# Offsets and masks spread over the partitions: by DMA from DRAM in fp32, or by matmuls on three bf16 parts

## Chip, cores and metric

One core of one Trainium2 chip runs the kernel. The metric is device time in microseconds, the median over several executions. All tensors are fp32 except where another type is named.

## What is computed

The input x is (8, 64, 16, 16). Two stages follow each other, each with a group normalisation of 32 groups and a residual.

```python
x = x + local_attention(_gn(x))        # 3x3 windows, 8 heads, a gate
x = x + relu(_mdcn(_gn(x)))            # modulated deformable 3x3 convolution
# _mdcn: om = conv3x3(x, w_om) + b_om  -> 108 rows: dy, dx, mask for 4 groups x 9 taps
py = h - 1 + ki + dy ; px = w - 1 + kj + dx
v  = bilinear(x[group], py, px) * sigmoid(mask)
out = einsum('ogck,bgckhw->bohw', w_dcn, v)
```

The change is in the second stage.

## The kernel before

Each engine has its own program; they meet at semaphores. The first stage ends at about 50 us, and the second normalisation and the offset convolutions follow.

**Offsets.** The convolution that gives offsets and masks runs in five pieces (`PIECES`: one image, one image, then two images each), six tap steps each (`convolve`, L1167), and leaves 108 rows in PSUM: 36 mask rows, 36 y rows and 36 x rows. ACT takes a piece out with its bias and puts tanh of half the mask rows in place (`offsets`, L592 and L594). DVE cuts the piece into three bf16 parts whose sum is the fp32 value, and takes the largest magnitude (`offset_part`, L876 to L886). SP stacks the three parts of a kind under one another in `stack_x`, `stack_y`, `stack_m` (L384 to L391).

**Sampling without a gather.** A sample is a product of hat functions: haty(row distance) times hatx(column distance). For every image i of 8 and every tap m of 9 (step t = 9 i + m, 72 steps) there are
- `select_x` (PE, L1232): for two taps at once, the x offset of each deformable group on its partitions, by a 0/1 matrix `selx` against the stacked parts, which also adds the column's own position. It goes to PSUM bank 5. ACT makes the hat from it, Abs (L628) and then Relu of 1 minus it (L630), into one of `HX` = 6 buffers.
- `select_y` (PE, L1218): the same for y, three slices an image (one, two and two pairs of taps), into PSUM bank 7; then Abs (L615) and Relu (L620) on ACT, and on 64 partitions the low half of an fp16 split on POOL (`low_y`, L478, L481, L485; the very first slice on DVE).
- `spread_mask` (PE, L1201 and L1207): the masks, six slices for each two images, into bank 7, and a copy out of it by ACT (L606).
- `spread_y` (PE, L1247): the y hats of the step, spread over the 128 partitions as three quarters of 256 columns, in two column halves, into banks 0 and 1 or 2 and 3 by turns.
- `multiply` (DVE, L915): the spread rows times the column weights, 768 columns, into one of 12 places of `smp`.

**Products.** Products of `smp` with the transposed image windows (PE, `block_of_products`, L1273, banks 4 and 6) sum up the samples; DVE multiplies them with the mask (`values`, L929, three parts an image), the weights are applied by `final` (PE, L1316), and DVE finishes an image (L942, L936). SP sends it out.

**Order.** The order on each engine is written out by hand in `sampling`. On PE, step t first does the spread of step t + 1, then select_x on even t, then blocks of products at m = 6, 7, 8 of the image and m = 0, 2, 3 of the next, the convolution of piece 3 within image 0 and of piece 4 within image 3 (`LAST_CONV`), window transposes, select_y for the next image at m = 2, 6, 8, mask slices where `MASKS` says so, and `final` at m = 5. Bank 7 is shared by select_y and the mask slices, and `bank7_free` waits for ACT to have taken the last one out. ACT follows the same order.

**If offsets are large**, further passes follow with other rows; in the run shown `choice` gives one pass.

Of the kernel before, what the change touches and what calls it, by code (L numbers as in the profile page):

```python
# [12 lines left out]
TAPS = 9  # L13
# [8 lines left out]
OM = 3 * DG * TAPS  # L22
ND = DG * TAPS
STACK = 3 * ND
# [25 lines left out]
UNITS = T // 2  # L50
HX = 6
LEAD = 2
SIDE = STRIPS // 2
# [13 lines left out]
MSLOT = 3 * BANK + 3 * HW  # L67

MASKS = [{4: (0, 0), 5: (0, 1), 7: (0, 2)}, {0: (0, 3), 1: (0, 4), 3: (0, 5), 5: (1, 0), 7: (1, 1)},
         {0: (1, 2), 3: (1, 3), 5: (1, 4), 7: (1, 5)}, {0: (2, 0), 3: (2, 1), 5: (2, 2), 7: (2, 3)},  # L70
         {0: (2, 4), 3: (2, 5)}, {0: (3, 0), 3: (3, 1), 5: (3, 2), 7: (3, 3)}, {0: (3, 4), 3: (3, 5)}, {}]


PIECES = [(0, 0, HW), (0, HW, BANK), (1, 0, BANK), (2, 0, BANK), (3, 0, BANK)]
PIECE_OF = {0: 0, 1: 1, 2: 2, 4: 3, 6: 4}
CONV_BANK = [4, 0, 6, 6, 4]
PAIRS_AT = {(0, m): (2 + m, 4) for m in range(6)} | {(1, 2): (8, 6)}
PARTS_AT = {(0, m + 1): (2, m) for m in range(5)} | {(1, m + 2): (3, m) for m in range(5)} | {(4, m): (4, m) for m in range(5)}
# [3 lines left out]
CHUNK, VALS, SLICES = 3, 3, 6  # L82
# [9 lines left out]


def seventh(i, m):

    at = i * STEPS + m - 1
    while at >= 0:
        i, m = divmod(at, STEPS)
        if m in SEL_Y and i + 1 < B:
            return "y", 3 * (i + 1) + SEL_Y[m] + 1  # L100
        if m in MASKS[i]:
            c, part = MASKS[i][m]
            return "m", SLICES * c + part + 1
        at -= 1
    return "y", 3


def bass_local_attention_then_deformable_conv(nc, x, cf, wom, sel16, rows16, out):
# [8 lines left out]
    with ExitStack() as ctx:  # L117
# [19 lines left out]
        selx = sb("selx", [STACK + 2, TAPS * P], bf16)  # L137
        own = sb("own_group", [P, DG])
        shiftbias = sb("shiftbias", [P, SHIFTS])
        sely = sb("s_sely", [STACK + 2, PAIRS * P], bf16)  # L140
        selm = sb("s_selm", [STACK + 2, 3 * P + 3 * C], bf16)
# [20 lines left out]

        conv_words = sb("conv_staged", [P, TAPSTEPS * OM + 2 * PAD])
        v = views(conv_words, ("womt", TAPSTEPS * OM), ("dup0", PAD), ("dup1", PAD))
        womt, dup = v["womt"], [v["dup0"], v["dup1"]]

        x_words = sb("x_parts", [P, 2 * N + P + 3 * BANK + BANK])
        v = views(x_words, ("xin", N), ("x2", N), ("beyond", P), ("parts", 3 * BANK), ("rest", BANK))
# [56 lines left out]
        def group_mask(rows):  # L225

            return own[:, :].unsqueeze(1).unsqueeze(3).to_broadcast([P, rows, DG, W])
# [119 lines left out]
        def _(sp):  # L347
# [33 lines left out]
            for p, piece in enumerate(PIECES):  # L381
# [10 lines left out]
                if p == 1:  # L392
                    odd_pairs(0)
# [1152 lines left out]
```

## Time and profile before

| | |
|---|---|
| median of 3 runs | 194.14 us (194.06 to 194.34) |
| the profiled execution's own time | 194.37 us |
| its span, first to last instruction | 192.4 us |
| PE busy | 171.5 us, 89% |
| DVE busy | 152.3 us, 79% |
| ACT busy | 103.8 us, 54% |
| POOL busy | 86.6 us, 45% |
| moved by DMA | 7.66 MB |
| granted TensorE clock, mean | 0.999 |

The span leaves out about 2 us around the instructions. PE is TensorE, DVE VectorE, ACT ScalarE, POOL GpSimd, SP the engine that issues most DMAs. A share of busy time is an average over stages with different limits, so the stretches of the sampling are read one by one. PE's busy time counts overlapping matmuls from first to last; the chain of waits tells what a group of them adds to the path.

### The profile page before, as it was taken

What the parts mean: (1) busy time and instruction counts of PE and PEld (TensorE: products, weight loads), DVE (VectorE), ACT (ScalarE), POOL (GpSimd) and SP (SyncE); (2) the same over time, 40 slices, a digit from 0 to 9 for tenths busy, and PEclk for the clock granted to TensorE, in tenths of its full rate; (3) what the DMA queues carried; (4) which work ended last, traced back from release to release, by engine and by line L of the source; (5) the groups of instructions that cost most, each with busy time, mean ns of one, the idle gap of its engine ahead of it and who ended that gap; (6) DMA issues with size and microseconds to landing.
All of it is one profiled execution on the core that took longest, in us unless ns stands there. A gap on an engine that the chain in (4) does not pass through costs nothing.

```text
span 192.4 us, 4617 instructions
## 1 busy us (share of the span) xinstructions
PE 171.5 (89%) x1818; PEld 119.0 (62%) x1818; DVE 152.3 (79%) x258; ACT 103.8 (54%) x195; POOL 86.6 (45%) x103
## 2 busy tenths in 40 slices
PE   0598888979799989999989999999889999999990
PEld 0234434634257535557777999467668888998870
DVE  3999889993869789966889988428998897979920
ACT  1165086400007795559848878367848868686000
POOL 8608971974023076505806627304624617545000
PEclk9999999999999999999999999999999999999999
DMA  5951000000030114018141000000011100000001
GB/s 171 313 90 14 3 0 0 3 0 0 18 91 12 30 32 117 13 46 217 27 118 49 0 3 3 0 0 0 13 38 49 33 19 3 0 17 2 20 0 24
DMA packets 10325, 7.66 MB, mean 40 GB/s; under 512 B 5175, under 2 KB 8773, under 8 KB 10297
## 3 DMA queue, kind: packets, MB, share of 16 engines
q1 hardware_dynamic: 10201, 7.24, 14.7%
q8 instruction: 16, 0.26, 0.6%
q14 instruction: 12, 0.10, 0.2%
q0 software_dynamic: 96, 0.06, 0.1%
HBM read 2.82 MB, written 0.52 MB: 17 GB/s over the span
## 4 chain that ended last, share of the span: by engine, by line
PE 62%; DVE 17%; ACT 9%; issue 4%; DMA 3%; POOL 2%; SPq 0%; DVEq 0%; POOLq 0%
PE ps L1273 20%; PE ps L1247 11%; PE ps L1167 10%; PE ps L1316 6%; DVE smp_prod L778 4%; DVE smp_prod L804 3%; PE ps L1232 3%; PE ps L1099 3%; DMA kept<-in_cf 3%; PE ps L1218 2%; ACT disty L615 2%; PE ps L1184 2%; ACT haty L620 1%; PE ps L1027 1%; ACT hx_selx L628 1%
## 5 line engine op out<-in xcount | busy, mean ns | idle before, releaser
L915 DVE TENSOR_TENSOR smp_prod<-ps,hx_selx 128x768 f32<-128x768 f32 x72 | 67.4, 952 | 10.0 <-PE ps L1247 9.2
L1273 PE MATMUL ps<-smp_prod,windows_attention 128*64 128x192 f32 (+2 forms) x512 | 54.9, 337 | 0.1
L1273 PEld LDWEIGHTS ps<-smp_prod,windows_attention 128*64 128x64 f32 x512 | 38.3, 136 | 5.8 <-DVE windows_attention L900 0.4
L1247 PE MATMUL ps<-haty,by_rows 128*64 128x256 f16 x432 | 39.1, 274 | 1.3 <-DVE smp_prod L915 1.2
L478 POOL TENSOR_SCALAR disty<-disty 64x512 f32<-64x512 f32 (+1 forms) x23 | 14.0, 610 | 57.6 <-ACT haty L620 57.6
L1247 PEld LDWEIGHTS ps<-haty,by_rows 128*64 128x64 f16 x432 | 26.6, 109 | 6.4 <-issue 2.7
L628 ACT ACTIVATE hx_selx<-ps 128x512 f32<-128x512 f32 x36 | 21.3, 591 | 16.2 <-PE ps L1232 16.2
L485 POOL TENSOR_TENSOR haty<-disty,haty 64x512 f16<-64x512 f32 (+1 forms) x23 | 24.0, 1042 | 1.9
L1167 PE MATMUL ps<-conv_staged 128*108 128x512 f32 (+1 forms) x60 | 23.3, 521 | 0.8 <-ACT x_parts L592 0.6
L630 ACT ACTIVATE hx_selx<-hx_selx 128x512 f32<-128x512 f32 x36 | 22.7, 631 | 1.1
L929 DVE TENSOR_TENSOR vals_attw<-ps,windows_attention 128x384 f32<-128x384 f32 x24 | 13.3, 555 | 7.4 <-PE ps L1273 4.4
L615 ACT ACTIVATE disty<-ps 128x512 f32<-128x512 f32 (+1 forms) x24 | 12.5, 520 | 8.0 <-PE ps L1218 7.3
L1232 PE MATMUL ps<-stack_x,selx 110*64 110x256 bf16 x144 | 16.3, 272 | 0.0
L481 POOL TENSOR_SCALAR disty<-disty 64x512 f32<-64x512 f32 (+1 forms) x23 | 14.7, 638 | 1.9
L1167 PEld LDWEIGHTS ps<-conv_staged 128*108 128x108 f32 x60 | 9.5, 172 | 8.1 <-issue 5.9
L620 ACT ACTIVATE haty<-disty 128x512 f16<-128x512 f32 (+1 forms) x24 | 13.4, 559 | 0.8
L606 ACT COPY windows_attention<-ps 128x512 f32<-128x512 f32 (+1 forms) x24 | 11.2, 467 | 4.8 <-PE ps L1201 2.7
L592 ACT ACTIVATE x_parts<-ps,kept 108x256 f32<-108x256 f32 (+1 forms) x3 | 1.6, 538 | 21.9 <-PE ps L1167 21.9
L449 POOL TENSOR_TENSOR smp_prod<-smp_prod 128x1024 f32<-128x1024 f32 x4 | 9.3, 2357 | 6.0 <-DVE smp_prod L804 6.0
L1099 PE MATMUL ps<-smp_prod,kept 128*128 128x512 f32 x20 | 9.6, 611 | 1.6 <-POOL smp_prod L449 1.6
L804 DVE TENSOR_TENSOR smp_prod<-ps,windows_attention 128x1024 f32<-128x1024 f32 x9 | 10.5, 1213 | 0.1
L1232 PEld LDWEIGHTS ps<-stack_x,selx 110*64 110x64 bf16 x144 | 10.3, 110 | 0.0
(138 smaller groups left out, 244.5 us busy)
## 6 DMA issues: line engine op xcount, KB each, us to landing
windows_attention<-windows_attention SPq DMA_DIRECT2D x8, 256.0 KB, 3.8
x_parts<-in_x SPq DMA_DIRECT2D x2, 256.0 KB, 3.1
bcast<-in_bcast SPq DMA_DIRECT2D x2, 256.0 KB, 7.0
x2seq<-x_parts SPq DMA_DIRECT2D x4, 128.0 KB, 2.5
out<-x_parts SPq DMA_DIRECT2D x16, 32.0 KB, 2.0
vals_attw<-in_cf SPq DMA_DIRECT2D x1, 480.0 KB, 5.9
stack_m<-x_parts SPq DMA_DIRECT2D x12, 36.0 KB
kept<-in_cf SPq DMA_DIRECT2D x1, 390.5 KB, 5.2
```

What stands on the lines that cost most here:

```text
L485: nc.gpsimd.tensor_tensor(hi, d, hi, ALU.add).then_inc(s_loy, 1)
L615: nc.scalar.activation(d, bank(7)[:, 0:w], ACT.Abs).then_inc(s_absy, 1)
L620: nc.scalar.activation(haty[i % 2][:, YP[e] * HW:YP[e] * HW + w], d, ACT.Relu, bias=1.0, scale=-1.0).then_inc(s_hiy, 1)
L628: nc.scalar.activation(h, bank(5), ACT.Abs).then_inc(s_absx, 1)
L630: nc.scalar.activation(h, h, ACT.Relu, bias=1.0, scale=-1.0).then_inc(s_hatx, 1)
L804: nc.vector.tensor_tensor(grid(prod[:, t * N:(t + 1) * N]), grid(bank(PB[pos % 3], 2)), shifted(vpad, t), ALU.mult).then_inc(s_pv, 1)
L915: nc.vector.tensor_tensor(pairs, rows, cols.unsqueeze(1).to_broadcast([P, QUARTERS, HW]), ALU.mult).then_inc(s_mult, 1)
L1099: ins = nc.tensor.matmul(bank(2 + c), ident, prod[:, t * N + c * BANK:][:, 0:BANK], start=(t == 0), stop=(t == 6))
L1167: ins = nc.tensor.matmul(bank(CONV_BANK[p])[0:OM, lo:hi], womt[:, k * OM:(k + 1) * OM], shifted(dup[h], 3 * ky + 2 * single)[:, j:j + (hi ...
L1232: ins = nc.tensor.matmul(bank(5)[h * C:(h + 1) * C, k * HW:(k + 1) * HW], selx[:, tap * P + h * C:tap * P + (h + 1) * C], stack["x"][:, i ...
L1247: ins = nc.tensor.matmul(ps[h * C:(h + 1) * C, at:at + HW], by_matrix(a, QUARTERS - 1 - k)[:, h * C:(h + 1) * C], haty[i % 2][:, p * HW:(p ...
L1273: return nc.tensor.matmul(dst[:, at:at + strips * 3 * SP].rearrange("p (s k n) -> p s k n", k=3, n=SP), rows, sampled(i, ki, m, first, str ...
```

## The change

The three bf16 parts, the stacks, the select matmuls and the mask matmuls are taken out.
- The convolution's weights are put in another order on POOL (`womo`), so that its rows come out as 36 mask rows, 40 y rows (two parities of taps, four groups, five pairs) and 36 x rows, 112 in all (`PLACED`). DVE adds the position of the sample (`where`, `shiftcol`, the bias for the first two pieces, straight from PSUM) in fp32 (`place`).
- SP writes the rows to a DRAM tensor `placed_rows`, waits for that write, and reads them back with a source that repeats, so that each row lands on all the partitions that need it: `expand_x` (three taps, 128 x 768), `expand_y` (one image, 128 x 1280), `expand_masks` (one image, four transfers of 64 partitions). For the masks of the first two images there is an extra write after ACT.
- ACT's Abs reads these tiles, with a bias per partition for what depends on the partition; units of x have three taps, four buffers. Mask rows hold tanh + 1, and the final weights are halved.
- Banks 4, 5 and 7 come free of the selects: `spread_y` goes through three pairs of banks (`SPREADS`) and runs two steps ahead (`AHEAD`).
- The order on partitions in windows and by_rows changes from group by column to column by group.
- Piece 4 is convolved in bank 6, at m = 2, 3, 4 of image 3, and `final` at m = 5 waits for its exit from PSUM.
- SP's program interleaves the expansions, the window copies (`odd_pairs`) and the output.

```diff
-UNITS = T // 2
-HX = 6
+UNIT = 3
+UNITS = T // UNIT
+UW = UNIT * HW
+HX = 4
 LEAD = 2
+AHEAD = 2
+SPREADS = 3
...
+            def place(p):
...
+                if p < DIRECT:
+                    dve.wait_ge(s_conv, p + 1)
+                    src, add = bank(CONV_BANK[p])[0:PLACED, lo:hi], direct[:, :]
+                else:
                     dve.wait_ge(s_om, p + 1)
+                    src, add = om[n // 2][:, n % 2 * BANK + lo:n % 2 * BANK + hi], shiftcol
+                nc.vector.scalar_tensor_tensor(placed[:, n * BANK + lo:n * BANK + hi], src, add, where[:, lo:hi], ALU.add,
+                                               ALU.add).then_inc(s_placed, 1)
...
+            def expand_x(u, it):
+
+                i, k = divmod(u, UNIT)
+                reach(sp, s_mult, UNIT * (u - HX) + UNIT, it)
+                sp.dma_start(cols_of(u), rows_of(i, ND + NY + UNIT * k, [[0, 2 * W], [TAPS * HW, DG], [1, UW]])
+                             ).then_inc(s_xrows[u % HX], 16)
+
+            def expand_y(i, lo, hi, signal, it):
+
+                reach(sp, s_loy, 3 * (i - 1), it)
+                sp.dma_start(disty[:, i % 2 * YI + lo:i % 2 * YI + hi],
+                             rows_of(i, ND + lo // HW, [[0, 2 * WROWS], [YI, 2 * DG], [1, hi - lo]])).then_inc(signal, 16)
+
+            def expand_masks(i, it):
+
+                reach(sp, s_vals, VALS * (i - 1), it)
+                for ki in range(2):
+                    sp.dma_start(masks_at(i, slice(ki * C, (ki + 1) * C), 0, UW),
+                                 rows_of(i, 3 * ki, [[0, CG], [TAPS * HW, DG], [1, UW]])).then_inc(s_mrows[i % 2], 16)
...
+            write(0)
+            sp.wait_ge(s_wrote[0], 16)
+            expand_y(0, 0, HW, s_yfirst, 0)
+            expand_x(0, 0)
+            expand_y(0, HW, YI, s_yrows[0], 0)
+            expand_x(1, 0)
+            write(1)
+            expand_x(2, 0)
+            for p in range(DIRECT):
+                write_mask(p)
+            for p in range(DIRECT):
+                sp.wait_ge(s_wrotem[p], 16)
+                expand_masks(p, 0)
+            sp.wait_ge(s_wrote[1], 16)
+            expand_y(1, 0, YI, s_yrows[1], 0)
+            odd_pairs(0)
             for i in range(B):
-                sp.wait_ge(s_y, i + 1)
-                send(i)
+                if i == 0:
+                    write(2)
+                if i + 1 < B:
+                    if i + 1 == 2:
+                        sp.wait_ge(s_wrote[2], 16)
+                    expand_x(UNIT * (i + 1), 0)
+                if 0 < i < J:
+                    odd_pairs(i)
+                if i == 1:
+                    write(3)
+                if i == 4:
+                    write(4)
+                if i + 1 < B:
+                    expand_x(UNIT * (i + 1) + 1, 0)
+                if i and i + 1 < B:
+                    expand_masks(i + 1, 0)
...
+                    expand_y(i + 2, 0, YI, s_yrows[i % 2], 0)
+                if i + 1 < B:
+                    expand_x(UNIT * (i + 1) + 2, 0)
+                if i:
+                    sp.wait_ge(s_y, i)
+                    send(i - 1)
...
             def hat_x(v, it):
...
-                h = hx[:, v % HX * BANK:(v % HX + 1) * BANK]
-                reach(act, s_selx, v + 1, it)
-                reach(act, s_mult, 2 * (v - HX) + 2, it)
-                nc.scalar.activation(h, bank(5), ACT.Abs).then_inc(s_absx, 1)
+                h = cols_of(v)
+                reach(act, s_xrows[v % HX], 16 * (v // HX + 1), it)
+                nc.scalar.activation(h, h, ACT.Abs, bias=firstx).then_inc(s_absx, 1)
...
             def spread_y(t, it):
...
-                reach(pe, s_mult, t - 1, it)
+                reach(pe, s_mult, t - SPREADS + 1, it)
...
-                    at = t % 2 * 2 * BANK + k * HW
+                    at = t % SPREADS * 2 * BANK + k * HW
...
-                    if t + 1 < T:
-                        spread_y(t + 1, it)
-                    if t % 2 == 0 and t // 2 + LEAD < UNITS:
-                        select_x(t // 2 + LEAD, it)
+                    if t + AHEAD < T:
+                        spread_y(t + AHEAD, it)
```

## Rows read from the trace of the kernel before

**Rows 1.** The page, part 1: busy time of each engine, share, instructions.
```profile
PE 171.5 (89%) x1818; PEld 119.0 (62%) x1818; DVE 152.3 (79%) x258; ACT 103.8 (54%) x195; POOL 86.6 (45%) x103
```

**Rows 2.** Stretches: length, busy us of PE, PEld, DVE, ACT, POOL, clock, DMA share, GB/s.
```profile
56.10:67.30 11.20, 11.17 (x60) 7.15 (x60) 9.76 (x24) 6.81 (x12) 1.77 (x3) 1.00 0.07 18
67.30:89.50 22.20, 21.42 (x172) 11.67 (x174) 17.94 (x22) 15.84 (x30) 11.58 (x12) 1.00 0.28 71
89.50:103.10 13.60, 12.99 (x178) 9.97 (x172) 12.41 (x20) 10.61 (x21) 5.74 (x10) 1.00 0.38 95
103.10:114.50 11.40, 11.40 (x176) 10.76 (x173) 10.30 (x16) 9.29 (x19) 5.31 (x8) 1.00 0.05 13
114.50:132.80 18.30, 18.20 (x196) 13.26 (x193) 10.49 (x16) 11.56 (x21) 6.51 (x10) 1.00 0.00 1
132.80:146.70 13.90, 12.56 (x178) 9.67 (x176) 13.70 (x20) 9.11 (x18) 6.57 (x9) 1.00 0.10 27
146.70:159.50 12.80, 12.80 (x186) 10.61 (x184) 10.79 (x19) 10.19 (x19) 6.55 (x10) 1.00 0.11 28
159.50:171.30 11.80, 11.80 (x182) 11.06 (x178) 10.29 (x16) 9.04 (x18) 6.01 (x9) 1.00 0.03 8
171.30:182.30 11.00, 11.00 (x157) 9.69 (x155) 10.01 (x15) 4.85 (x8) 4.40 (x6) 1.00 0.04 10
182.30:192.40 10.10, 4.91 (x60) 3.98 (x56) 1.69 (x5) 0.00 (x0) 0.00 (x0) 0.97 0.05 11
```

**Rows 3.** Chain that ended last, 156 to 166.6: start, us, what.
```profile
157.25 0.22 PE ps L1218 x4
157.47 0.33 PE ps L1247 x6
157.80 0.22 PE ps L1232 x4
...
159.00 0.11 PE ps L1207 x2
```

**Rows 4.** Timeline of DVE, fifth image: first and last of five offset instructions.
```profile
133.66 1.30 DVE L876 CAST x_parts<-conv_staged 108x512 bf16<-108x512 f32 x1
...
141.53 0.67 DVE L886 TENSOR_REDUCE amax<-conv_staged 108x1 f32<-108x512 f32 x1
```

**Rows 5.** Groups by line and shape, 146.7 to 182.3: busy us, mean ns, idle before.
```profile
L630 ACT ACTIVATE hx_selx<-hx_selx 128x512 f32<-128x512 f32 x12 | 7.6, 631 | 0.4
...
L485 POOL TENSOR_TENSOR haty<-disty,haty 64x512 f16<-64x512 f32 x6 | 7.0, 1159 | 0.5
...
L481 POOL TENSOR_SCALAR disty<-disty 64x512 f32<-64x512 f32 x6 | 3.7, 618 | 0.5
...
L620 ACT ACTIVATE haty<-disty 128x256 f16<-128x256 f32 x2 | 0.8, 418 | 0.1
```

**Rows 6.** Two stretches with full DMA engines: loads from DRAM, then copies within SBUF.
```profile
6.00:8.00 2.00, 1.05 (x3) 0.93 (x4) 1.76 (x7) 0.30 (x1) 0.66 (x1) 1.00 1.01 379
88.00:90.00 2.00, 2.00 (x28) 1.37 (x27) 0.95 (x2) 1.97 (x4) 1.77 (x2) 1.00 0.94 246
```

**Rows 7.** Timeline of SP's queue: start, time to issue.
```profile
73.19 0.53 SPq L378 DMA_DIRECT2D windows_attention<-windows_attention  x1
```

**Rows 8.** DMA issues by tile: count, KB each, median us from issue to landing.
```profile
out<-x_parts SPq DMA_DIRECT2D x16, 32.0 KB, 2.0
```

**Rows 9.** Timeline of all engines around the first multiply.
```profile
58.54 1.38 DVE L709 TENSOR_SCALAR tall<-x_parts,pair,rstd 128x256 f32<-128x256 f32 x4
58.92 0.47 ACT L592 ACTIVATE x_parts<-ps,kept 108x256 f32<-108x256 f32 x1 [21.89 <-PE ps L1167]
...
67.31 0.96 DVE L915 TENSOR_TENSOR smp_prod<-ps,hx_selx 128x768 f32<-128x768 f32 x1
...
70.94 1.11 PE L1167 MATMUL ps<-conv_staged 128*108 128x512 f32 x2 [0.55 <-ACT x_parts L592]
```

**Rows 10.** Timeline of POOL before its second rstd.
```profile
54.04 1.02 POOL L459 TENSOR_TENSOR rstd<-vareps,minushalf 128x4 f32<-128x4 f32 x1 [8.59 <-DVE vareps L706]
```

More of the change, by code:

```diff
@@ new lines, in rows_of, with rows_to, by_image, cols_of @@
+        def rows_of(i, first, dims):
+            start = placed_rows[i, first, 0:HW]
+            return bass.AP(start.tensor, start.offset, dims)
+        def rows_to(p, rows):
+            n, lo, hi = PIECES[p]
+            i = 2 * n + lo // HW
+            return placed_rows[i:i + (hi - lo) // HW, rows].rearrange("i r n -> r i n")
+        def by_image(t):
+            return t.rearrange("r (i n) -> r i n", n=HW)
+        def cols_of(u, rows=slice(0, P)):
+            return hx[rows, u % HX * UW:(u % HX + 1) * UW]
@@ L279, in bass_local_attention_then_deformable_conv, with masks_at @@
+        def masks_at(i, rows, lo, hi):
+            return masks[rows, i % 2 * MW + lo:i % 2 * MW + hi]
+        def mask_of(i, part):
+            at = i % 2 * MW + (part * HF if part < 2 else UW)
+            first = masks[:, at:at + HF]
+            return bass.AP(first.tensor, first.offset, [first.ap[0], [SP, SIDE], [HW, 3], [1, SP]])
         s_x = [sem("s_x0"), sem("s_x1")]
[L280 removed]
+        s_cst, s_wom, s_consts = sem("s_cst"), sem("s_wom"), sem("s_consts")
@@ L363, in _ @@
-            for k in "xym":
-                sp.dma_start(stack[k][STACK:STACK + 2, :].bitcast(u16), rows16["x" if k == "x" else "y"]).then_inc(s_rows, 16)
+            for part in range(2):
+                first = sel16["bcast"][part * C, DG * P:3 * DG * P]
+                width = sel16["bcast"].shape[1]
+                sp.dma_start(bcast[part * C:(part + 1) * C, 0:2 * DG * P],
+                             bass.AP(first.tensor, first.offset, [[width, WROWS], [WROWS * width, WROWS], [1, 2 * DG * P]])
+                             ).then_inc(s_byload, 16)
@@ new lines, in _ @@
+            constant(column[rows_x, 0:1].bitcast(u16), sel16["selx"][STACK + 1, 0:1], [[0, DG], [P, TAPS], [1, 1]])
+            for part in range(2):
+                rows = slice(part * C, (part + 1) * C)
+                constant(column[rows, 1:2].bitcast(u16), sel16["selx"][STACK + 1, P:P + 1], [[1, W], [0, DG], [1, 1]])
+                constant(column[rows, 2:3].bitcast(u16), sel16["sely"][STACK + 1, 0:1], [[1, WROWS], [0, WROWS], [1, 1]])
+            at, width = kept.shape[1] - 5 - 1, cf.shape[1]
@@ L1303, in block_of_products @@
                 tiles = [(2, 0), (2, 1)] if kind == 2 else [(0, kind), (1, kind)]
-                products(i, tiles, bank(6 if kind == 1 else 4), part, it)
+                products(i, tiles, bank(6 if kind == 1 else 7), part, it)
             def final(i, it):
```

438 lines of the change are left out of this document (191 added, 247 removed).

## The prediction

> **What bounds the kernel now.** I read the page's shares first [rows 1]: TensorE (PE) is busy 89% of the span and VectorE (DVE) 79%, so both limits lie close together. The table by stretches [rows 2] says where each one holds. Its cuts are mine: the first multiply by the column weights (67.3 us), and then the end of each image's mask product at step 8. The last images (159.5 to 182.3) have PE busy in every microsecond, 11.8 and 11.0 us an image, with DVE at 10.3 and 10.0. In the second and the fifth image (89.5 and 132.8) it is DVE that is full, because it cuts the offsets into bf16 parts there. The fourth (114.5) is PE again, with a convolution of the offsets in it. The first (67.3) takes 22.2 us. Before 56.1 nothing is changed that the path goes through. The chain of waits [rows 3] gives what one operation costs PE on the path, which the mean duration of a matmul does not, since the two 64-column halves overlap: a row spread 0.33 us, a select_x 0.22, a select_y 0.22 (half for the one-tap slice), a mask slice 0.11 (twice that where it has 512 columns instead of 256).
>
> **PE.** The change removes select_x, select_y and spread_mask. An image holds 4.5 select_x (0.99 us), three select_y (0.11 + 0.22 + 0.22 = 0.55) and three mask slices (0.33, or 0.66 in every other image): 1.9 to 2.2 us. The sixth image then needs 12.8 - 2.2 = 10.6, the seventh 11.8 - 1.9 = 9.9, the eighth, without a select_y, 11.0 - 1.3 = 9.7.
>
> **DVE.** It keeps nine multiplies, three mask products, two finishing operations. Busy it is at 10.3 us in the seventh image, and that becomes the floor, as PE falls below it. Spreads three deep instead of two let PE run one further ahead, so that the waits of DVE for a spread (0.5 to 0.6 us each, two in such an image) should mostly go. I take 10.9 an image, DVE's busy time and half a microsecond of what is left of the waits. In the images where the offsets are handled, five instructions per piece (four part cuts and one maximum, 4.1 us in the fifth image with their queueing [rows 4], about 2.9 without) become two, an addition and a maximum. The maximum took 0.67 [rows 4], and the addition has the same 512 columns, so 1.35: 1.5 to 2.7 us less.
>
> **ACT.** 36 pairs of Abs and Relu on 512 columns become 24 pairs on 768. A Relu took 631 ns at 512 and 418 at 256 [rows 5], 0.84 ns a column, so 0.85 us at 768: 1.70 a unit and 5.1 an image, plus 3.3 for the y hats. That is 8.4 in an image of 10.9. The mask copies out of bank 7 go, and with them PE's waits for that bank. ACT now reads what a DMA puts down, so it waits on landings, in the order of its program.
>
> **The transfers** are the new work. Per image: three x units of 128 x 768 x 4 B = 0.393 MB, y 128 x 1280 x 4 = 0.655, masks 64 x (2 x 768 + 2 x 640) x 4 = 0.721, together 2.56 MB, all issued by SP, where [rows 2] has shares of 0.03 to 0.11. How fast they run no row shows, since nothing is spread from DRAM over partitions with a repeated source. The bounds: loads from DRAM in rows of 2 to 4 KB ran at 379 GB/s when the engines were full, and copies inside SBUF at 246 GB/s at share 0.94 [rows 6]. These transfers are loads from DRAM in rows of 2.5 to 5 KB, nearest to 379; I work with that: 6.7 us of an image. At 246 it is 10.4, which just fits. SP needs 0.5 us an issue [rows 7], ten issues an image, 5 to 6 us, also hidden. Landing after issue costs about 2.0 us besides [rows 8].
>
> Is an image fed in time? The masks of the next image wait for the values of step 4, 0.45 of an image P in. Behind them on SP stand the y rows and the third x unit: 1.77 MB, 4.7 us, with issue and landing 7.2. ACT then does that unit, the first y slice, two more units, the second y slice: 1.7 + 0.8 + 1.7 + 1.7 + 1.2 = 7.1, and POOL's three operations on it take 0.62 + 0.62 + 1.16 = 2.4 (the first is as wide as the second) [rows 5]. The spread that needs it comes at the start of the image after next: 2P = 0.45P + 16.7, P = 10.8. That is my 10.9, so it closes without slack. I add 1.0 us in all for waits it leaves, between 0 and the 5 us of the rival below.
>
> **The start.** Before: ACT takes piece 0 out of PSUM at 58.92, the first multiply is at 67.31, and PE goes on with the next convolution at 70.94, released by ACT, which has just taken piece 2 out [rows 9]. After: DVE is in its normalisation until 59.9 [rows 9], adds piece 0 until 60.3 and SP writes it to DRAM (issue 0.7, landing 2.0: 63.0). The first y rows (0.13 MB, issue 0.5 and landing about 2) land at 65.3, the first x unit at about 66.6, its two operations end at 68.3: the first multiply comes 1.0 us late. ACT then has window copy, y slice, x unit, y slice (0.6 for the copy, as wide as a Relu of [rows 5], + 1.2 + 1.7 + 1.2 = 4.7) and piece 2 (0.7), which is out at 73.7 and PE's next convolution starts 2.8 us late. From there to the end of the first image PE is the limit, and it loses the selects and mask slices (about 1.9 us) and the stalls on bank 7. I put the two first stretches together at +0.6.
>
> **Weight permutation, constants, by_rows** before 56.1: POOL has 8.6 us of idle time ahead of its second rstd [rows 10], the four permuting copies of up to 216 columns cost some 2 us there by its operations of 512 [rows 5], and the twelve small loads are issued when SP is idle. Cost nothing; if one came late, the convolutions start late by as much. The Identity scaling in place of copies, the other order of channels in copies and stagings have the same number of elements: nothing.
>
> **The sum**, stretch by stretch [rows 2]: start and first image +0.6; second 13.6 to 12.0, -1.6; third 11.4 to 10.9, -0.5; fourth 18.3 to 16.2 (PE 18.2 less 2.0), -2.1; fifth 13.9 to 12.2, -1.7; sixth 12.8 to 11.5 (the search for the farthest offset stays), -1.3; seventh -0.9; eighth 11.0 to 10.5, -0.5; the tail -1.0, as PE is no longer behind with products that need only the first six taps when the last multiply ends. Together -9.0, with the feed's +1.0: -8.0. The profiled execution took 194.37, 0.23 above the median of 194.14: 186.1 us for the median.
>
> **The rivals.**
> A. The feed is late (0.19). The place is ACT's in-order wait for the x unit behind masks and y rows. For: the equation above closes with nothing over. Against: the row of 379. At 300 GB/s the 1.77 MB need 1.2 us more, P = 11.6, about 0.8 in each of six images: 190 to 191. At 246, P = 12.4, nearly the old time.
> B. Slower (0.15): the transfers do not keep the rate because sixteen engines read the same few rows at once. Place: every expansion. Price: the old mean image is (182.3 - 89.5) / 7 = 13.3 us, so the point is 2.56 MB / 13.3 = 193 GB/s. At half of 379, 190 GB/s, an image takes 13.5 even where nothing else is late, the first one a few microseconds more: 195 to 199. For: the range between my two rows already goes down to 246, neither with repeated sources. Against: the sources are short and the destinations spread evenly.
> The Trainium skill, "DMA: Bandwidth & Descriptors", section "Latency and other measured facts", says that streams which step through HBM in lock step at large pitches got about half the rate of others (103 against 207 GB/s). Here, where the images' rows lie 9 KB apart and not at such a pitch, a loss of that size would bring about rival B. The rows show no such loss at 379, but no transfer of this shape either.
> C. The start eats more (0.06). PE has nothing from about 70.4 to 73.5 and the granted clock, 1.00 in all stretches but the last [rows 2], may fall to the lower level (1.2 GHz). A 512-wide pair of the convolution takes 1.1 us [rows 9]; the six at half speed cost some 6 us more, and 4 if the clock comes back on the way: 190 to 192.
> The Trainium skill, "TensorE: Matmul & The Clock Gate", part 1, says that an idle TensorE goes back to half its clock. In this trace PE never stood long enough in the sampling for the rows to agree or disagree.
> D. It does not do what it says (0.05): DVE was the limit all along and its waits stay; what PE gives back is lost in DMA waits, within 0.2%.
> E. More than forecast (0.04): under 182.
>
> **How the numbers follow.** The forecast, 182 to 189.5, has 0.51. Measurement of this kernel can tell about 0.2% from no change. Faster: 0.51 + 0.04 + A 0.17 + C 0.06 = 0.78. Same: D 0.05. Slower: B 0.15 and 0.02 of A. The range leaves out E and the slow half of B: 182.0 to 195.5. Within the forecast alone the range is 182 to 189.5.
>
> **What would show it.** In the changed profile: images six to eight of 10.5 to 11 us with DVE at 95% busy and PE below 95%; DMA share 0.6 to 0.7 from the first image on and about 230 GB/s; the first multiply at 68.3; ACT's Abs on the x unit waiting for a DMA rarely. ACT waits of more than a microsecond in each image would be A; a DMA share near 1.0 with below 240 GB/s, B; a clock below 1.00 near 72 us, C. Wrong outright would be a DVE multiply that takes longer than 0.95 us beside the DMA traffic, of which I took none: 72 multiplies at 5% more are 3.4 us.

## The result: 5.7% slower

The changed kernel took 205.51 us (median of 4 runs, 204.33 to 206.37), the kernel before on the same chip 194.24: ratio 1.0573, 95% interval 1.0517 to 1.063. The forecast was 186.1 within 182.0 to 195.5. The profiled execution took 204.33 us with a span of 202.2. (Some executions of this program come out longer at a lower clock: medians and extremes count them, ratios and the differences in microseconds between two runs do not.) Page of the changed kernel, parts 1 and 2:

```profile
PE 160.4 (79%) x1546; PEld 102.8 (51%) x1546; DVE 142.8 (71%) x243; ACT 95.7 (47%) x149; POOL 85.8 (42%) x108
...
PEclk9999999999999969859999999999999999999998
```

Both big engines did less, as forecast (PE 171.5 to 160.4 us, DVE 152.3 to 142.8 [rows 1]), in a longer span. In most images that got longer no engine is full over the whole image, so something is waited for; the exception is the DMA engines in the third image (share 1.02). The stretches of the changed kernel, cut at the same events as in [rows 2] (first multiply, then the mask product at step 8 of each image; columns as there):

```profile
56.30:70.20 13.90, 10.23 (x46) 6.73 (x46) 7.96 (x18) 7.39 (x13) 0.00 (x0) 1.00 0.44 116
70.20:96.50 26.30, 21.54 (x128) 11.16 (x130) 15.63 (x19) 16.71 (x26) 10.18 (x12) 0.81 0.73 197
96.50:107.90 11.40, 11.10 (x150) 8.72 (x148) 11.18 (x18) 8.45 (x13) 4.92 (x8) 1.00 0.75 208
107.90:122.60 14.70, 10.69 (x146) 8.21 (x144) 9.86 (x16) 6.85 (x10) 6.01 (x9) 1.00 1.02 248
122.60:142.70 20.10, 16.36 (x158) 10.06 (x156) 10.01 (x16) 11.97 (x19) 6.99 (x11) 1.00 0.73 185
...
154.80:168.10 13.30, 10.82 (x148) 8.43 (x145) 10.43 (x19) 9.31 (x14) 6.97 (x11) 1.00 0.77 209
168.10:179.70 11.60, 10.51 (x146) 8.29 (x144) 9.83 (x16) 7.88 (x12) 5.71 (x9) 1.00 0.76 211
179.70:191.60 11.90, 10.12 (x136) 7.80 (x134) 9.65 (x15) 2.77 (x4) 4.60 (x6) 1.00 0.14 43
```

Start and first image end at 96.5 where they ended at 89.5: +7.0. The next seven give -2.2, +3.3, +1.8, -1.8, +0.5, -0.2, +0.9, and the tail +0.5; the sum is 9.8, the difference of the spans. Against the forecast's terms that is 6.4 us too much up to the end of the first image, 7.7 in the third and fourth together, 3.9 in the sixth to eighth and 1.5 in the tail; the second and fifth came out as forecast or a little better. In the eighth image neither PE (10.12 of 11.90) nor DVE (9.65) is full, and no DMA is either (share 0.14). What stands between them shows in the chain of waits, grouped (us in total, times, longest), and in the DMA issues (count, KB each, median us from issue to landing):

```profile
ACT hx L738 <- DMA hx<-placed_rows: 29.3, 10, 6.3
...
DVE vals_attw L1032 <- PE ps L1335: 21.0, 17, 3.9
...
PE ps L1309 <- POOL haty L599: 10.2, 6, 3.4
```

```profile
hx<-placed_rows SPq DMA_DIRECT2D x24, 384.0 KB, 5.4
disty<-placed_rows SPq DMA_DIRECT2D x7, 640.0 KB, 5.5
```

The x units land 5.4 us after issue. For a unit by itself the forecast had 2.0 [rows 8] and the unit's own 1.0; for the third unit of an image it counted from the issue of the masks ahead of it, 7.2. ACT waits for them ten times. PE waits six times in a row spread (L1309) for POOL's low half of the y hats (L599), and DVE, in its mask product (L1032), for PE's products (L1335). One of the six, by the timeline of the changed kernel (start, us, engine, line; [idle before]):

```profile
178.07 0.71 ACT L728 ACTIVATE disty<-disty,offset 128x512 f32<-128x512 f32 x1
...
178.81 0.63 ACT L731 ACTIVATE haty<-disty 128x512 f16<-128x512 f32 x1
...
179.53 0.61 POOL L592 TENSOR_SCALAR disty<-disty 64x512 f32<-64x512 f32 x1 [3.10 <-ACT haty L731]
180.22 0.62 POOL L595 TENSOR_SCALAR disty<-disty 64x512 f32<-64x512 f32 x1
180.93 1.15 POOL L599 TENSOR_TENSOR haty<-disty,haty 64x512 f16<-64x512 f32 x1
...
182.22 0.52 PE L1309 MATMUL ps<-haty,by_rows 128*64 128x256 f16 x6 [1.78 <-POOL haty L599]
...
182.55 1.05 PE L1335 MATMUL ps<-smp_prod,windows_attention 128*64 128x288 f32 x9
...
183.72 0.56 DVE L1032 TENSOR_TENSOR vals_attw<-ps,windows_attention 128x384 f32<-128x384 f32 x1 [2.25 <-PE ps L1335]
```

Read from the end: DVE stands 2.25 us for products, which stand behind a spread that waits for POOL, which waited for ACT. DVE's last multiply was over at 181.47, so what the products read of it was there. The spread stands ahead of them because it is issued two taps ahead, and ACT came to the slice at 178.07 because it works through its list in order: it had waited 3.56 us for an x unit until 172.04, and did three units and the slices between them without a pause from then on. That landing was late by itself. For the same unit, SP's first transfer ahead of the unit, and ACT's instruction that waits for the unit:

```profile
163.09 1.18 SPq L437 DMA_DIRECT2D windows_attention<-placed_rows  x2
...
172.04 0.94 ACT L738 ACTIVATE hx<-hx,offset 128x768 f32<-128x768 f32 x1 [3.56 <-DMA hx<-placed_rows]
```

Masks, y rows and the third x unit took 8.95 us where the forecast had 7.2. Two stretches from the issue of the masks to such a landing, the one of the fourth image's third unit and this one (columns as in [rows 2]):

```profile
115.50:129.20 13.70, 7.96 (x113) 6.48 (x113) 7.14 (x11) 8.17 (x12) 6.19 (x9) 1.00 0.96 225
163.10:172.00 8.90, 7.30 (x107) 6.09 (x107) 7.12 (x14) 5.14 (x8) 5.14 (x8) 1.00 0.89 241
```

For the third image's third unit it was 11.9 us. There and in the first of these stretches the queue also carried window copies and the next x unit, about 3 MB where the forecast counted 1.77.

The start, in the same view:

```profile
72.96 1.19 SPq L437 DMA_DIRECT2D windows_attention<-placed_rows  x2
...
78.01 0.59 SPq L430 DMA_DIRECT2D disty<-placed_rows  x1
```

ACT:

```profile
84.51 0.51 ACT L728 ACTIVATE disty<-disty,offset 128x256 f32<-128x256 f32 x1 [6.23 <-DMA disty<-placed_rows]
```

PE:

```profile
81.29 1.11 PE L1272 MATMUL ps<-conv_staged 128*112 128x512 f32 x2
85.99 1.12 PE L1289 MATMUL ps<-kept,windows_attention 128*128 128x128 f32 x4 [3.59 <-ACT windows_attention L718]
...
87.82 2.05 PE L1272 MATMUL ps<-conv_staged 128*112 128x512 f32 x2
```

SP waits for the masks' write until 72.96, issues eight mask transfers and only then the y rows of the second image. ACT waits 6.23 us for them with a window copy behind it, PE 3.59 us for that copy. After this idle time the granted clock is down (0.81 over the stretch from 70.2; the page's PEclk has a 6 in the slice from 70.8, after a first pause of 2.4 us, then 8 and 5 in those from 80.9 and 85.9), and the pair of convolution matmuls takes 2.05 us where it took 1.11: the level of 1.2 GHz. (The Trainium skill, "TensorE: Matmul & The Clock Gate", part 1, says that an idle TensorE goes back to half its clock; this trace agrees.)

### The profile page after: what moved, and what is told of

It is laid out like the page before. It is cut to its first block, busy times and chain, and to the rows that moved or that the text cites. A ratio compares the mean times of both kernels' runs of the same rounds, so it can differ in the third digit from the quotient of the medians.

```text
span 202.2 us, 3958 instructions
## 1 busy us (share of the span) xinstructions
PE 160.4 (79%) x1546; PEld 102.8 (51%) x1546; DVE 142.8 (71%) x243; ACT 95.7 (47%) x149; POOL 85.8 (42%) x108
## 4 chain that ended last, share of the span: by engine, by line
PE 28%; DVE 22%; DMA 19%; ACT 10%; POOL 8%; issue 6%; SPq 4%; DVEq 0%; POOLq 0%
PE ps L1335 10%; DMA hx<-placed_rows 8%; PE ps L1309 6%; PE ps L1272 4%; DMA placed_rows<-x_placed 4%; DVE smp_prod L888 4%; DMA disty<-placed_rows 3%; DVE smp_prod L914 3%; POOL haty L599 3%; DVE smp_prod L1020 3%; DMA kept<-in_cf 3%; PE ps L1204 3%; ACT hx L738 3%; ACT disty L728 2%; PE ps L1378 2%
## 5 line engine op out<-in xcount | busy, mean ns | idle before, releaser
L1020 DVE TENSOR_TENSOR smp_prod<-ps,hx 128x768 f32<-128x768 f32 x72 | 65.6, 949 | 3.5 <-ACT hx L740 1.8
L1335 PE MATMUL ps<-smp_prod,windows_attention 128*64 128x192 f32 (+2 forms) x512 | 53.6, 337 | 2.7 <-DMA windows_attention<-windows_attention 2.3
L1309 PE MATMUL ps<-haty,by_rows 128*64 128x256 f16 x432 | 37.5, 280 | 16.1 <-POOL haty L599 10.2
L1335 PEld LDWEIGHTS ps<-smp_prod,windows_attention 128*64 128x64 f32 x512 | 36.8, 137 | 9.4 <-DMA windows_attention<-windows_attention 2.6
L1309 PEld LDWEIGHTS ps<-haty,by_rows 128*64 128x64 f16 x432 | 23.9, 111 | 29.3 <-DVE smp_prod L1020 15.8
L738 ACT ACTIVATE hx<-hx,offset 128x768 f32<-128x768 f32 x24 | 22.3, 930 | 29.4 <-DMA hx<-placed_rows 29.3
L1032 DVE TENSOR_TENSOR vals_attw<-ps,windows_attention 128x384 f32<-128x384 f32 x24 | 13.3, 555 | 21.0 <-PE ps L1335 21.0
L1272 PE MATMUL ps<-conv_staged 128*112 128x512 f32 (+1 forms) x60 | 25.7, 561 | 0.1
L599 POOL TENSOR_TENSOR haty<-disty,haty 64x512 f16<-64x512 f32 (+1 forms) x23 | 24.9, 1083 | 1.9
L740 ACT ACTIVATE hx<-hx 128x768 f32<-128x768 f32 x24 | 20.3, 844 | 0.8
L728 ACT ACTIVATE disty<-disty,offset 128x512 f32<-128x512 f32 (+1 forms) x24 | 15.3, 637 | 6.2 <-DMA disty<-placed_rows 6.2
L1272 PEld LDWEIGHTS ps<-conv_staged 128*112 128x112 f32 x60 | 10.2, 187 | 8.0 <-issue 6.7
L595 POOL TENSOR_SCALAR disty<-disty 64x512 f32<-64x512 f32 (+1 forms) x23 | 13.1, 568 | 1.9
L914 DVE TENSOR_TENSOR smp_prod<-ps,windows_attention 128x1024 f32<-128x1024 f32 x9 | 10.5, 1212 | 0.1
L1005 DVE COPY windows_attention<-ps 128x512 f32<-128x512 f32 x4 | 2.8, 692 | 11.0 <-PE ps L1289 11.0
L538 POOL TENSOR_TENSOR smp_prod<-windows_attention 128x512 f32<-128x512 f32 x6 | 7.0, 1207 | 5.0 <-ACT windows_attention L658 5.0
L1147 PE MATMUL ps<-windows_attention,vals_attw 128*128 128x512 f32 x16 | 7.8, 618 | 0.4 <-DVE windows_attention L854 0.4
```

The lines of the kernel that those rows point to most:

```text
L599: nc.gpsimd.tensor_tensor(hi, d, hi, ALU.add).then_inc(s_loy, 1)
L728: nc.scalar.activation(d, d, ACT.Abs, bias=firsty if isinstance(it, int) else ybias[:, :]).then_inc(s_absy, 1)
L738: nc.scalar.activation(h, h, ACT.Abs, bias=firstx).then_inc(s_absx, 1)
L740: nc.scalar.activation(h, h, ACT.Relu, bias=1.0, scale=-1.0).then_inc(s_hatx, 1)
L914: nc.vector.tensor_tensor(grid(prod[:, t * N:(t + 1) * N]), grid(bank(PB[pos % 3], 2)), shifted(vpad, t), ALU.mult).then_inc(s_pv, 1)
L1020: nc.vector.tensor_tensor(pairs, rows, cols.unsqueeze(1).to_broadcast([P, QUARTERS, HW]), ALU.mult).then_inc(s_mult, 1)
```

## The experiments

The theory after reading (O): the order of three lists costs, ACT's (y slices behind x units that have not landed), PE's (a waiting spread ahead of the products) and SP's (what is wanted first issued last). In the earlier expectations it is still called F, the order of the feed, and has no word yet on the lead of the spreads. The rivals: the DMA rate with repeated sources, or the amount (R), and the ring of four x units (K). Ratios are to the kernel before on the same chips, with 95% intervals; its medians lay between 194.2 and 194.6.

**The rate by itself.** A kernel with nothing but six transfers each of: x rows with a repeated source, the same size from distinct rows, y rows repeated (5 KB packets), y distinct, y repeated in halves, SBUF to SBUF. It computes nothing of the reference, and each kind was timed once.

> The kernel does none of the reference's work: it copies x to the output and times transfers by themselves, six of a kind in a row and a wait behind each kind: (1) 128 x 768 from DRAM with each of 4 rows repeated 32 times, as the x units are; (2) the same size with 128 distinct rows; (3) 128 x 1280 with 8 rows repeated 16 times, as the y rows are; (4) the same with distinct rows; (5) the y rows in two transfers of 640 columns; (6) 128 x 1024 inside SBUF. Theory R (repeated sources are slow): kinds 1 and 3 run at 250 GB/s or less, kinds 2 and 4 at 350 or more. Theory F (the rate is not the matter, the order of the feed is): 1 and 2 alike near 380, 3 and 4 alike; a packet of 5120 B may be slower than one of 3072 B (372 against 121 ns in the changed kernel's trace), and then kind 5 beats kind 3.

Stretches with full engines, in that order (the last two columns are DMA share and GB/s):

```profile
16.00:22.00 6.00, 0.00 (x0) 0.00 (x0) 1.00 0.94 322
26.00:32.00 6.00, 0.00 (x0) 0.00 (x0) 1.00 0.98 292
36.00:50.00 14.00, 0.00 (x0) 0.00 (x0) 1.00 1.02 238
55.00:62.50 7.50, 0.00 (x0) 0.00 (x0) 1.00 1.00 382
68.00:80.00 12.00, 0.00 (x0) 0.00 (x0) 1.00 1.05 253
84.50:90.00 5.50, 0.00 (x0) 0.00 (x0) 1.00 1.02 405
```

Neither expectation fits whole. A repeated source costs the y rows over a third of their rate (238 against 382), the x rows nothing (322 against 292). An image's 0.655 MB of y take 2.75 us instead of 1.73: the term of rate was 1 us an image too small for y alone. 238 is still well over the 193 GB/s at which rival B decided.

**Masks fetched for two images only.** The later images multiply by the masks of the first two, which leaves work out; from the third image on, 28% of an image's expanded bytes are gone.

```
-                if i and i + 1 < B:
-                    expand_masks(i + 1, 0)
...
-                    reach(dve, s_mrows[i % 2], 16 * 4 * (i // 2 + 1), it)
+                    reach(dve, s_mrows[i % 2], 16 * 4, it)
```

> The masks are fetched for the first two images only; images 2 to 7 multiply with the masks of the first two, so this kernel leaves out 4.3 MB of the 20.4 MB spread over the partitions, and SP's wait for the values of step 4. Theory F (the third x unit and the y rows stand behind the masks in SP's order): images six to eight come down to 10.9 us or less, third and fourth by 3 each, 205.5 - 9 = 196 to 197 us. Theory R (all transfers share a rate that is the bound): 28% less data, so images three and four come down by as much as F says, but six to eight, at a share of 0.77, by 1 at most: 199 to 201.

203.44 us, 1.0431 (1.0362 to 1.05), slower than either theory expected. Three microseconds of eleven came back: the masks' bytes alone are not the main cause. In its trace ACT still waits 22.6 us in 9 for x units, 4.7 of them in the sixth image for a unit that SP issued at 158.65, as soon as the multiply that frees its buffer in the ring of four had ended.

**The start's order.** The second image's y rows ahead of the masks, and its masks moved into the loop over the images.

```
-            for p in range(DIRECT):
-                sp.wait_ge(s_wrotem[p], 16)
-                expand_masks(p, 0)
             sp.wait_ge(s_wrote[1], 16)
             expand_y(1, 0, YI, s_yrows[1], 0)
+            for p in range(DIRECT):
+                sp.wait_ge(s_wrotem[p], 16)
+            expand_masks(0, 0)
...
-                if i and i + 1 < B:
+                if i + 1 < B:
                     expand_masks(i + 1, 0)
```

> Only SP's order at the start changes: the y rows of the second image go out before the masks of the first, and the masks of the second image after the fifth x unit. All work is done. Theory F: ACT's wait of 6.2 us for those y rows goes, and with it PE's wait of 3.6 us and the lower clock behind it: the first image is 4 to 6 us shorter, 200 to 201 us. Theory R: the same bytes have to pass, 1 us at most: 204.5 to 205.5.

201.93 us, 1.0344 (1.0316 to 1.0372): 3.9 us back. At the start it is 5.6, as read (the first image's mask product at 90.42 instead of 95.98); in that profile the fourth and eighth image, 22.2 and 14.1 us, are each some 2 us longer than in the changed kernel.

**The y hats first.** From the second image on, ACT does the three y slices of the next image together, ahead of the x units. SP's list is as it was.

```
+                    if i and m == 0 and i + 1 < B:
+                        for e in range(3):
+                            distance_y(i + 1, e, it)
                     if t % UNIT == 0 and t // UNIT + LEAD < UNITS:
                         hat_x(t // UNIT + LEAD, it)
-                    if m in SEL_Y and i + 1 < B:
+                    if m in SEL_Y and i == 0:
```

> Only ACT's order changes: from the second image on, the three y slices for the next image are done at the start of an image, ahead of the x unit on which ACT waits. All work is done. Theory F: PE's waits for POOL's low halves (10.2 us in six) go, six to eight come to about 11 us each: 199 to 201 us. Theory R: the x units land no sooner and the images keep their length: 204 to 206.

195.96 us, 1.0024 (0.9985 to 1.0063): 10.1 us back without a byte less, more than expected, and the slowest of its ten executions (198.89) is 5.4 us under the fastest of the changed kernel. ACT now waits 29.1 us in 6 for y rows, about as long as it waited for x units before, and 7.0 for x units (the profile is of that slowest execution); a wait of the same length in another place of the list costs far less.

**A ring of six x units.** `HX = 4` to `HX = 6`.

> Only HX goes from 4 to 6, so SP may issue an x unit six taps' multiplies earlier. All work is done. Theory F as it now stands (a unit v is issued when unit v - 4 is multiplied, lands 5.4 us or 4.5 taps later, and ACT does the y slices behind it in order): ACT's waits for x units (29.3 us in ten) fall to below 10, PE's waits for POOL's low halves too, 197 to 199 us. My older reading (the third unit stands behind masks and y rows on the queue): the unit is still issued behind them, 204 to 205. Theory R (the rate): no change, 205 to 206.

204.85 us, 1.0569 (1.0487 to 1.065): no difference, a miss for F, which had expected 197 to 199. The ring alone is not the cause. In its trace the third units of the sixth and seventh image still start on ACT 9.4 and 9.0 us after the issue of the masks. So this run leaves the queue's delay and the run without most masks leaves the ring; both taken away together, in the old order of ACT, were not run.

**Start, ACT's order and early rows together.** Here SP also issues the y rows behind the first x unit of an image instead of behind its masks, and waits for the write of the fourth piece's offset rows in the second image instead of the third.

> Order alone, with the same bytes and four buffers: the start order of e2, the y slices first on ACT as in e3, and the y rows of the image after next issued at the start of an image, ahead of the masks, since POOL is done with their buffer by then. All work is done. Theory F: the waits of ACT for y rows that e3 shows (29.1 us in six) go, 190 to 193 us. Theory R: the queue is as full as before, 195 to 197.

194.3 us, 0.9902 (0.9867 to 0.9937): level with the kernel before by the median, 1% under by the ratio. With the ring of six on top:

> e5 with HX = 6. All work is done. Theory F: with both causes of late feed gone the images come to the forecast of the prediction, 10.9 us, and the first to about 23: 186 to 189 us. Theory R: the transfers hold at about 250 GB/s, 10.2 us of each image, and any unevenness shows: 190 to 193.

194.26 us, 0.9945 (0.9905 to 0.9986), no gain over the run without it. K falls here too, and F's 186 to 189 did not come.

**Two deep.** The changed kernel with the spreads as before the change, one tap ahead in two slots.

```
-AHEAD = 2
-SPREADS = 3
+AHEAD = 1
+SPREADS = 2
...
-            spread_y(1, 0)
```

> The changed kernel with two pairs of PSUM banks for the row spreads and one step ahead, as before the change; all else is as changed. Theory F: the third pair is what let DVE run on while PE waited for the y hats, without it each such wait comes through: 207 to 209 us. Rival: PE waits at the same places whatever its depth, since the late y hats stop it in order: 205 to 206.

198.91 us, 1.0212 (1.0157 to 1.0267). Both expectations missed: they had it slower or the same, and it is 6.6 us faster. The three-deep spreads, which the forecast counted as a gain, cost that much here. PE's waits for POOL fall from 10.2 us in 6, DVE's for products from 21.0 in 17:

```profile
PE ps L1309 <- POOL haty L599: 5.9, 5, 2.6
...
DVE vals_attw L1032 <- PE ps L1335: 2.8, 2, 1.4
...
DVE smp_prod L1020 <- PE ps L1309: 20.6, 19, 2.8
```

The last line is the other side: DVE now waits 20.6 us for spreads where it waited 0.9, so its waits for these two together are no shorter. What fell besides PE's waits are DVE's for window transposes (11.0 to 7.6), for the final matmuls (4.2 to 1.9) and for a piece of the offsets (2.8 to 0.3).

**Three slots, one tap ahead.** This tells the third slot from the place in PE's order: `AHEAD = 1`, `SPREADS = 3`.

> The changed kernel with three slots in PSUM kept and the spreads issued one tap ahead instead of two. Theory O: the place in TensorE's order is what cost, so the time is that of two deep, 198 to 200 us, or up to 1 us less since the third slot takes away waits of a spread for a multiply. Rival S (the cost is in the third slot itself, by the banks it takes from the windows or by the place of the start's second spread): 204.5 to 206.5.

198.81 us, 1.016 (1.0127 to 1.0193), the same as two deep within the intervals. The lead costs, the slot does nothing.

**The orders with one tap ahead**, in two slots and in three.

> The orders of the run that changed start, ScalarE and transfers together (194.3 us) with the row spreads two deep and one tap ahead. Theory O (a spread two taps ahead costs because it waits for late y hats and stands in front of the products): with the y hats early there is little late left for it to wait for, so most of the 6.6 us that two deep gave back alone is already had, and the time is 191 to 194. Rival P (two ahead costs by itself, the distance between TensorE and VectorE and not the late hats): the 6.6 us come back in full, 187.5 to 189. Rival K (three deep does help once the hats are in time): 196 to 199.

> The three orders with three slots kept and one tap ahead. Theory O: within 1 us of the same orders two deep (191 to 194), under it by the waits of PEld for a multiply, which were 7.1 us in 12 in the two-deep run and mostly hidden. Rival P: 187 to 189.5.

193.36 us, 0.9901 (0.9873 to 0.9929), and 194.1 us, 0.9943 (0.9913 to 0.9973); with two taps ahead it was 0.9902. Once the hats are in time, neither the lead nor the slot matters. That is what O says, and the further 6 us of P (two ahead costs by itself) did not come.

**What keeps these from the forecast?** In the two-slot run the seventh and eighth image took 9.9 and 10.3 us, under the forecast's 10.9 and 10.5, but the second took 17.4 and the third 13.1. In the second the DMA engines are full from 98.0 to 108.6 (share 0.99) and the granted clock is 0.84 there. First the amount again, then the masks' place, behind the third x unit.

> The best orders (three orders, two deep: 193.4 us), with the masks fetched for the first two images only, so that 28% of the expansion's bytes are gone; the later images multiply by the masks of images 0 and 1, which leaves work out. Under the old order this gave back 2 us of 11. Theory M (with the order mended, the amount is what is left: the transfers of an image's end now run at share 1.03 in the sixth image): 188 to 190.5. Rival N (what is left is waits by order and the start, not the amount): 192 to 193.5.

> The same best orders with every byte, and the masks of the next image issued behind its third x unit instead of ahead of it. They are wanted at step 8 of that image, the x units and y rows sooner. Theory M: the bytes that stand in front of what is wanted first are moved back, 0 to 3 us less than 193.4: 190.5 to 192.5. Rival N: no change, 192.5 to 193.7. A third way, that the masks then come late themselves, would show as VectorE waiting for a DMA ahead of the mask product and give 194 or more.

Without most masks (work left out again) 192.88 us, 0.9917 (0.9891 to 0.9944): no difference from 193.36. With the masks moved back 196.51, 1.0126 (1.0087 to 1.0166), slower by 3.6 us: a miss for both theories. In its profile VectorE does not wait for masks; the third image takes 3.2 us more (16.3) and the sixth 2.0 less (11.3). The two executions profiled are only 0.5 us apart (195.53 and 195.05), so these stretches don't account for the 3.6, and why it is slower stays open.

The chain of the two-slot run then showed the next list, SP's own (start, us, what):

```profile
97.92 7.88 DMA placed_rows<-x_placed
105.80 0.02 issue
105.82 0.54 SPq L424
```

SP waits in order for the write of the offset rows, which lands 7.9 us after its issue behind copies, an x unit and masks, and the third x unit stands behind that wait; ACT waits 6.5 us for it. In these orders this wait stood an image earlier than anything needs it. TensorE also waited 5.8 us in 2 for the copies of odd window pairs. Both moved, and the write of that piece was put ahead of the y rows:

```
@@ the loop over images on SyncE
-                if i + 2 < B and i not in (0, 4):
-                    expand_y(i + 2, 0, YI, s_yrows[i % 2], 0)
-                if 0 < i < J:
-                    odd_pairs(i)
                 if i == 1:
                     write(3)
+                if i == 2:
+                    sp.wait_ge(s_wrote[3], 16)
+                if i + 2 < B and i not in (0, 4):
+                    expand_y(i + 2, 0, YI, s_yrows[i % 2], 0)
...
-                if i == 1:
-                    sp.wait_ge(s_wrote[3], 16)
                 if i + 1 < B:
                     expand_x(UNIT * (i + 1) + 2, 0)
+                if i + 1 < J:
+                    odd_pairs(i + 1)
```

> The orders of the 193.4 us run, with SyncE's list changed once more: the copies of odd window pairs an image earlier, behind the third x unit, the write of the fourth image pair's offset rows ahead of the y rows, and the wait for that write moved from the second image to the third. In the 193.4 us run that wait stood ahead of the third x unit of the second image (the write landed 7.9 us after its issue behind masks and copies, and ScalarE waited 6.5 us for the unit), and TensorE waited 5.8 us in 2 for the copies. Theory Q (what is left above the forecast is waits in the list of one queue): the second image falls from 17.4 to 13 to 15 us and the third from 13.1 to 11.5 to 12.5, 187.5 to 191. Rival M (the engines behind the queue are full, so that what goes earlier delays something else): 192 to 194.

190.21 us, 0.9697 (0.9645 to 0.9748): 3% under the kernel before, the best version; all six of its executions (187.61 to 191.22) lie below every one of the kernel before (194.15 up). It differs from the changed kernel by the order of the lists and the two constants of the spreads; all of the change but the third spread slot and the second step of lead is in it. Its three moves were made together, so which of them gave what is not shown. The second image's clock is 1.00, where it was 0.90 in the run before, so part of the gain there may be clock. Its stretches (second, third, fourth, then sixth to eighth image):

```profile
91.00:103.40 12.40, 11.35 (x154) 8.80 (x152) 11.96 (x17) 10.05 (x16) 10.71 (x14) 1.00 0.98 249
103.40:113.70 10.30, 10.30 (x146) 8.23 (x144) 9.96 (x16) 7.47 (x11) 6.25 (x9) 1.00 1.05 256
113.70:132.30 18.60, 16.24 (x158) 10.09 (x156) 10.55 (x15) 12.58 (x19) 6.41 (x10) 1.00 0.96 230
...
143.40:157.30 13.90, 11.33 (x152) 8.57 (x150) 10.66 (x20) 8.66 (x13) 6.24 (x9) 1.00 0.99 268
157.30:167.10 9.80, 9.80 (x140) 7.78 (x138) 9.67 (x15) 8.17 (x12) 6.26 (x9) 1.00 0.63 164
167.10:177.40 10.30, 10.30 (x144) 8.12 (x142) 9.96 (x15) 1.78 (x2) 0.00 (x0) 1.00 0.16 51
```

## Why the prediction was wrong, step by step

**PE and DVE, the floors: right in size.** PE's work fell by 11.1 us, and by 14.5 in the fastest version, whose mean clock is nearer to full (0.984 against 0.97), where 1.9 to 2.2 an image were forecast; DVE's fell by 9.5. Fed in time, the third image runs in 10.3 us (forecast 10.9), the seventh in 9.8 (10.9), the eighth in 10.3 (10.5), with DVE busy for 97 to 99% of it and PE for all. (The sign "PE below 95%" did not come: PE's busy time counts overlapping matmuls, and here it fills the image.) The multiply stayed at 0.949 us beside the transfers, so that way of being wrong did not come.

**The feed equation, P = 10.8 "without slack", +1.0 us: the step that failed most.** Its shape was right, with the place, ACT's in-order wait for the third x unit; every leg of it can be read in the changed kernel. The spreads at the start of the sixth, seventh and eighth image are at 157.49, 170.00 and 182.22, so two images take 24.7 us and P is 12.4. The masks go out 5.6 us in, which is 0.45 P as forecast. The queue then takes 8.95 (forecast 7.2), ACT 7.4 (7.1), and POOL with the hand-over 2.8 (2.4). The term that was mis-sized is the queue's, and in the third and fourth image it was far worse, 11.9 and 13.7 for the same 7.2. It was worked out at 379 GB/s with nothing else on the queue; the stretches ran at 225 to 241, and in those two images window copies and the next x unit shared the engines. With no slack in the equation each microsecond of it makes P 0.65 us longer (1 / 1.55). Rival A had this mechanism, and its figure at 246 GB/s, P = 12.4, is the measured one. It called that "nearly the old time"; but the start, and the third and fourth image with their window copies, put the total well above it. That y slices stand behind that landing in ACT's list is what turned a late queue into a late image: with the slices moved ahead of it, and every byte still fetched, 10.1 us came back.

**Three deep, -0.5 us an image: wrong in sign.** This is the other failed step. The forecast priced it as slack for DVE, and DVE's waits for spreads did go (0.9 us left of 9.2); but they came back as waits for products (21.0), since a spread that has to wait for a hat now stands further ahead of the products in PE's one list. One step of lead less gave 6.6 us, with the slot or without it. An estimate from the forecast's own equation says why the hats bind: one tap less of lead moves the spread's deadline by P/9, so that 2.11 P = 0.45 P + 19.1 and P = 11.5 instead of 12.4; the sixth to eighth image two deep took 11.9, 11.2 and 11.7. With the hats in time the lead was worth nothing either way.

**The rate, 379 GB/s: mis-sized.** Alone the y rows ran at 238 and the x rows at 322, and in the kernel stretches with a DMA share of 0.98 or more moved 248 to 268. At 250, 2.56 MB take 10.2 us, as the lower bound had it: it just fits. The rate works through the queue's leg above. Rival B's time came out (and more); what it says of repeated sources is true of the y rows, but no full stretch fell to its 193 GB/s, and 28% fewer bytes gave 2.9 us back, and nothing resolvable once ACT's order was mended. How much fewer bytes and a longer ring give together in the old order was not run. (The Trainium skill, "DMA: Bandwidth & Descriptors", section "Latency and other measured facts", has half rate for rows at large pitches; the nearest here is 238 against 382, a factor of 0.62, for repeated y rows only.)

**The start, +0.6: measured +7.0 with the first image.** The first multiply came at 70.23, not 68.3, as the first x unit was through ACT only at 70.13. The rest is the y rows of the second image behind eight mask transfers, and the lowered clock after PE's idle time, rival C's mechanism, which showed where it was placed (the slice from 70.8) and again after the pause before 85.99. The order of SP's list alone gave 3.9 back (5.6 by the end of the first image).

**ACT: a little low.** A pair on 768 columns took 0.930 + 0.844 = 1.77 us (forecast 1.70), the y slices 3.6 an image (3.3). It has the time; its order is what failed.

**The weights' permutation and constants at nothing: right, within 0.2 us.** The first convolution's addition is at 60.10 in the changed kernel (60.3 less its 0.4 was forecast).

**What the orders give together, and what is left.** Alone, the y hats' place gives 10.1 us, the lead 6.6, the start 3.9; together, with the y rows issued earlier besides, 12.6 of their 20.6. The first two share waits: a spread's lead costs only while hats are late. What is left between 190.2 and 186.1 sits in the fourth image (18.6 us, forecast 16.2), the sixth (13.9, forecast 11.5, with a wait of ACT for y rows of 6.6 us) and the tail (10.5, forecast 9.1). The experiments don't settle these. Y rows that can be issued only after an offset piece has been written are argued, not shown; and as the DMA engines are full in both of these images (shares 0.96 and 0.99), the amount is a rival again for what is left. It was tested without most masks only before these last moves.

## What to carry to other kernels

Where a DMA takes over what an engine made, its landing enters the in-order list of every engine that reads it. Write down, for each such list (the issuing queue's too), what stands behind each wait and who wants it first, with landings at what the loaded queue gives, everything on it counted: here 5.4 to 6.6 us for a unit counted at 3.0, and 9 to 14 for a group counted at 7.2. One step more of lead is a gain only if the leading instruction's inputs are ready; if not, it moves a wait ahead of work that could run. Test order and amount separately, and two limits that stand at the same place also together: here less data gave 1.4% and another order of the same data 8%.

## What the runs showed of the hardware

- In one timing of each kind, loads of 5 KB rows that sixteen partitions each take from the same source ran at 238 GB/s, in 2.5 KB halves at 253, and from distinct rows at 382. For 3 KB rows that 32 partitions share there was no such loss (322 against 292).
- Transfers within SBUF reached 405 GB/s alone, where [rows 6] had 246 beside other work.
- From issue to landing 384 KB took 5.4 us (median, 3.4 to 10.2) in the changed kernel and 6.6 in the fastest version. A longer landing is no sign of a slower kernel.
- ACT's Abs with a bias from a per-partition tile took 930 ns on 768 columns, the Relu beside it, with constants, 844.
